# A gated recurrence on one core: the update gate's recurrent product in half precision from a split state, behind the reset gate's, and VectorE's side work in another order

## What is computed

```python
vz = video @ C_z + b_z; vr = video @ C_r + b_r; vh = video @ C + b
xz = einsum('btd,de->bte', seq, W_z)   # xr with W_r, xh with W
def step(h, xs):
    z = sigmoid(xzt + h @ U_z + vz)
    r = sigmoid(xrt + h @ U_r + vr)
    hh = tanh(xht + r * h @ U + vh)
    h_new = (1.0 - z) * h + z * hh
    return (h_new, h_new)
out = x + (all h_new, by batch and time)
```

## Time and profile before

| | |
|---|---|
| median of three runs | 2472.28 us (2469.28 to 2473.05) |
| profiled execution, its own time | 2469.78 us |
| its span, first to last instruction | 2468.0 us |
| busy: PE, DVE, ACT, POOL | 97%, 63%, 32%, 26% |
| mean granted clock of TensorE | 0.991 |

### The profile page before, as it was taken

The page is one execution under the profiler, slowest core; times in us unless marked ns, Lnnn a source line. Parts: engine busy times, 40 slices in busy tenths (PEclk is TensorE's granted clock), DMA queues, the critical chain, the costliest instruction groups (busy, mean ns, idle before and its releaser), DMA issues.

```text
span 2468.0 us, 166186 instructions
## 1 busy us (share of the span) xinstructions
PE 2390.1 (97%) x74366; PEld 2074.1 (84%) x74366; DVE 1544.1 (63%) x6617; ACT 787.9 (32%) x2571; POOL 632.5 (26%) x1165
## 2 busy tenths in 40 slices
PE   2999999999999999999999999999999999999998
PEld 1888888888888888888888888888888888888887
DVE  3666656666566665666656666566665666666665
ACT  2333333333333333333333333333333333333322
POOL 0222222222222222222222222222222222222222
PEclk8999999999999999999999999999999999999999
DMA  9010110110101101101101111011011011011000
GB/s 192 22 39 22 39 39 22 39 34 26 40 22 38 39 21 40 38 21 39 38 23 38 31 29 38 23 38 39 22 38 40 21 39 38 22 38 38 21 21 21
DMA packets 145969, 87.90 MB, mean 36 GB/s; under 512 B 9024, under 2 KB 140608, under 8 KB 145216
## 3 DMA queue, kind: packets, MB, share of 16 engines
q1 hardware_dynamic: 145216, 76.84, 12.2%
HBM read 43.25 MB, written 33.55 MB: 31 GB/s over the span
## 4 chain that ended last, share of the span: by engine, by line
PE 96%; issue 1%; SPq 1%; DVE 1%; DMA 1%; ACT 0%; POOLq 0%; POOL 0%; DVEq 0%
PE banks L208 55%; PE p_bank L216 40%; DMA w_stage<-in_L_cond_W_z_dram 1%; SPq L120 0%; SPq L115 0%; SPq L126 0%; DVE h_t L473 0%; DVE w_top L394 0%; DVE taken L467 0%; PE p_bank L224 0%; ACT gate_c L324 0%; DVE state L471 0%; DVE w_lo L407 0%; ACT w_hi L311 0%; SPq L123 0%
## 5 line engine op out<-in xcount | busy, mean ns | idle before, releaser
L216 PE MATMUL p_bank<-w_hi,x_t 128*32 128x384 f16 x16384 | 1122.1, 327 | 7.1 <-issue 7.0
L208 PE MATMUL banks<-u,h_t 128*32 128x128 f32 x32768 | 1004.1, 274 | 18.7 <-issue 16.8
L208 PEld LDWEIGHTS banks<-u,h_t 128*32 128x32 f32 x32768 | 912.9, 110 | 73.5 <-issue 23.9
L216 PE MATMUL p_bank<-w_lo,x_t 128*32 128x384 f16 x8192 | 739.2, 327 | 0.5 <-issue 0.5
L216 PEld LDWEIGHTS p_bank<-w_hi,x_t 128*32 128x32 f16 x16384 | 510.2, 97 | 115.3 <-issue 9.9
L208 PE MATMUL banks<-u,reset_t 128*32 128x128 f32 x16384 | 554.4, 274 | 2.8 <-issue 2.3
L455 DVE TENSOR_TENSOR reset<-gate_r,state 128x64 f32<-128x64 f32 x1024 | 226.7, 221 | 509.6 <-ACT gate_r L319 509.6
L208 PEld LDWEIGHTS banks<-u,reset_t 128*32 128x32 f32 x16384 | 442.2, 109 | 87.1 <-DVE reset_t L457 35.8
L187 POOL TENSOR_TENSOR result<-x_nat,state 128x128 f32<-128x128 f32 x512 | 235.4, 460 | 939.6 <-DVE state L471 939.6
L181 POOL TENSOR_TENSOR kept<-keep,state 128x128 f32<-128x128 f32 x512 | 236.0, 461 | 875.3 <-ACT keep L321 875.3
L388 DVE SCALAR_TENSOR_TENSOR banks<-p_bank,x_down,base 128x128 f32<-128x128 f32 x1536 | 429.4, 341 | 6.3 <-PE p_bank L216 4.2
(11 more groups left out here) (39 smaller groups left out, 419.9 us busy)
## 6 DMA issues: line engine op xcount, KB each, us to landing
x_nat<-in_x_dram SPq DMA_DIRECT2D x256, 128.0 KB, 2.9
out_dram<-result SPq DMA_DIRECT2D x256, 128.0 KB, 2.7
c_w<-in_L_cond_C_r_dram SPq DMA_DIRECT2D x4, 256.0 KB, 6.4
c_w<-in_L_cond_C_z_dram SPq DMA_DIRECT2D x4, 256.0 KB, 9.1
c_w<-in_L_cond_C_dram SPq DMA_DIRECT2D x4, 256.0 KB, 11.8
w_stage<-in_L_cond_W_r_dram SPq DMA_DIRECT2D x4, 256.0 KB, 14.6
w_stage<-in_L_cond_W_z_dram SPq DMA_DIRECT2D x4, 256.0 KB, 16.6
w_stage<-in_L_cond_W_dram SPq DMA_DIRECT2D x4, 256.0 KB, 17.1
```

The lines of the kernel that those rows point to most:

```text
L208: last = nc.tensor.matmul(out[part(j)], turned[:, part(q)], weights[:, q, cols(j)], start=first and q == 0, stop=q == Q - 1, skip_group_ch ...
L216: last = nc.tensor.matmul(p_bank[k][part(j), 0:G * N], x_t[set_][:, c, part(q), a], w[b][:, :, q, cols(j)], start=f == 0, stop=f == GROUPS ...
```

## The change

The update gate's recurrent matrix `U_z` is scaled and split once at the start into two float16 halves, as the input matrices were before, and loaded ahead of them. In each step ScalarE rounds the turned state to float16 (`h_hi`), VectorE makes the remainder (`h_lo`), and TensorE forms the update product from three float16 products, 48 matmuls of 128 columns, behind the reset product; the third of them waits for `h_lo`. The scale is taken out again in ScalarE's two sigmoids. Around it the side work is laid out in another way: the seed of the next step's reset gate moves to the head of VectorE's step, ahead of `h_lo`; the other two seeds stay; the scale of x is made over three steps; x is turned one time step at a time, three steps ahead, behind the seeds; and ScalarE's two passes over x stand in different steps.

```diff
-    SUM_STEPS, TOTAL_STEP, SCALE_STEP, SPLIT_STEPS, TURN_STEPS = (0, 1), 2, 3, (3, 5), (5, 7)
+    SUM_STEPS, TOTAL_STEP, POWER_STEP, UP_STEP, DOWN_STEP = (7, 0), 1, 2, 3, 4
+    WHOLE_STEPS, HIGH_STEPS, TURN_AHEAD = (3, 5), (4, 6), 3
+    UZ = G
+    SPLITS = (UZ, R, Z, C)
...
+        uz = [sb(n, [P, Q, E], f16) for n in ("uz_hi", "uz_lo")]
+        h_hi, h_lo = sb("h_hi", [P, N], f16), sb("h_lo", [P, N], f16)
...
+            load_weights(u[:, Z], U_z, s_u_in[Z])
             for g, m in enumerate((W_r, W_z, W_h)):
                 load_weights(w_stage[:, g], m, s_w_in[g])
-            for g, m in enumerate((U_r, U_z, U_h)):
-                load_weights(u[:, g], m, s_u_in[g])
+            load_weights(u[:, R], U_r, s_u_in[R])
+            load_weights(u[:, C], U_h, s_u_in[C])
...
-                if t in SPLIT_STEPS and not (last and j == BODY - 1):
-                    k = SPLIT_STEPS.index(t)
+                if t in HIGH_STEPS and not (last and j == BODY - 1):
+                    k = HIGH_STEPS.index(t)
                     rest_of_x(k, 2 * n + 3 + k if first or last else pool.snap(2 * n + (3 + k)))
...
+            def update_product(out, now):
+                pe.wait_ge(h_hi_ready, now)
+                for a, b in PARTS:
+                    if a == 1:
+                        pe.wait_ge(h_lo_ready, now)
+                    for q in range(Q):
+                        for j in range(J):
+                            last = nc.tensor.matmul(out[part(j)], (h_hi, h_lo)[a][:, part(q)], uz[b][:, q, cols(j)],
+                                                    start=False, stop=q == Q - 1, skip_group_check=True)
+                return last
...
+            for m, g in enumerate(SPLITS):
+                pe.wait_ge(s_w_top, m + 1)
+                total(p_bank[0][:, G * N + 2 + g:G * N + 3 + g], all_sum, w_top[:, g:g + 1]).then_inc(s_w_total, 1)
+                pe.wait_ge(s_w_up, m + 1)
...
-                product(cell(k, Z), h_t, u[:, Z]).then_inc(z_mm, 1)
+                update_product(cell(k, Z), now).then_inc(z_mm, 1)
...
-                    if c == 0:
-                        sets = i * (STEPS // SET) + m + 1
-                        pe.wait_ge(x_t_ready, sets if last else pe.snap(sets))
+                    pe.wait_ge(x_t_ready, s + 3 if last else pe.snap(s + 3))
                     project(k, c, 0, BEFORE_C, m % 2)
...
+            def whole_x(n, k, before):
+                if before is not None:
+                    act.wait_ge(x_lo_ready, before)
+                nc.scalar.activation(x_whole[:], x_nat[n % BUFS][:, k * SET:(k + 1) * SET], ACT.Copy,
+                                     scale=x_up[n % 2][:]).then_inc(x_whole_ready, 1)
+
...
                 if turned is not None:
                     act.wait_ge(x_t_ready, turned)
-                if before is not None:
-                    act.wait_ge(x_lo_ready, before)
-                nc.scalar.activation(x_whole[:], tile, ACT.Copy, scale=x_up[n % 2][:])
-                nc.scalar.activation(x_parts[k][:, :, 0], tile, ACT.Copy, scale=x_up[n % 2][:]).then_inc(x_hi_ready, 1)
+                nc.scalar.activation(x_parts[k][:, :, 0], x_nat[n % BUFS][:, k * SET:(k + 1) * SET], ACT.Copy,
+                                     scale=x_up[n % 2][:]).then_inc(x_hi_ready, 1)
...
+            act.wait_ge(x_in[1], 16 * J)
+            sum_x(1, 0, 2)
+            for m, g in enumerate(SPLITS):
+                act.wait_ge(s_w_up, m + 1)
+                nc.scalar.activation(split_of(g, 0), stage_of(g), ACT.Copy, scale=w_up[:, g:g + 1]).then_inc(s_w_hi, 1)
...
+                act.wait_ge(h_t_ready, HALVES * (s + 1) if last else act.snap(HALVES * s + HALVES))
+                nc.scalar.activation(h_hi[:], h_t[:], ACT.Copy, scale=2.0 ** POW).then_inc(h_hi_ready, 1)
                 act.wait_ge(r_mm, now)
                 nc.scalar.activation(gate_r[:], cell(k, R), ACT.Sigmoid).then_inc(r_gate, 1)
                 act.wait_ge(z_mm, now)
-                nc.scalar.activation(keep[:], cell(k, Z), ACT.Sigmoid, scale=-1.0).then_inc(z_keep, 1)
-                nc.scalar.activation(gate_z[:], cell(k, Z), ACT.Sigmoid).then_inc(z_gate, 1)
+                nc.scalar.activation(keep[:], cell(k, Z), ACT.Sigmoid, scale=z_minus[:]).then_inc(z_keep, 1)
+                nc.scalar.activation(gate_z[:], cell(k, Z), ACT.Sigmoid, scale=z_down[:]).then_inc(z_gate, 1)
...
+                if t == SUM_STEPS[0] and more(2):
+                    b, u_ = divmod(j + 2, BUFS)
+                    act.wait_ge(x_in[u_], count(16 * J * (i * (BODY // BUFS) + b + 1)))
+                    sum_x(j + 2, 0, count(2 * n + 4))
+                if t == SUM_STEPS[1] and more(1):
+                    sum_x(j + 1, 1, count(2 * n + 3))
+                if t in WHOLE_STEPS and more(1):
+                    k = WHOLE_STEPS.index(t)
+                    if k == 0:
+                        act.wait_ge(x_scaled, count(n + 2))
+                    whole_x(j + 1, k, count(2 * n + (2 + k)))
+                if t in HIGH_STEPS and more(1):
+                    k = HIGH_STEPS.index(t)
+                    high_x(j + 1, k, count(BLOCK * n + (SET + SET * k)))
...
+            def power_x(k, n, count):
...
+                V.tensor_reduce(x_pow[k][:], p_bank[TOTAL_STEP % 2][:, G * N:G * N + 2], AX.X, ALU.add).then_inc(x_link, 1)
                 dve.wait_ge(x_link, count(4 * n + 1))
                 exponent_of(x_pow[k][:], x_pow[k][:]).then_inc(x_link, 1)
+
+            def up_x(k, n, count):
...
-                V.tensor_scalar(x_down[k][:], w_down[:], x_pow[k][:], None, ALU.mult).then_inc(x_link, 1)
-
-            def turn_x(k, sets):
+                V.tensor_scalar(x_down[k][:], w_down[:, 0:G], x_pow[k][:], None, ALU.mult).then_inc(x_link, 1)
+
+            def turn_x(k, c, sets):
                 dve.wait_ge(x_lo_ready, sets)
...
+                V.transpose(x_t[k][:, c].rearrange("p n a -> p (n a)").bitcast(i32),
+                            x_parts[k][:, cols(c)].rearrange("p n a -> p (n a)").bitcast(i32)).then_inc(x_t_ready, 1)
+
+            def seed(k, d, gates):
+                for g in gates:
                     last = V.scalar_tensor_tensor(cell(k, g), p_bank[k][:, cols(g)], x_down[d][:, g:g + 1], base[:, g],
                                                   ALU.mult, ALU.add)
-                last.then_inc(seeded, 1)
...
+                    if g == C:
+                        last.then_inc(seeded, 1)
+
...
+            def scales_of_z():
+                link(V.tensor_copy(z_down[:], w_down[:, UZ:UZ + 1]))
+                link(V.tensor_scalar(z_minus[:], z_down[:], -1.0, None, ALU.mult))
+                link(up_of(z_up[:], w_pow[:, UZ:UZ + 1], 2 * POW))
+                link(V.tensor_scalar(base[:, Z], base[:, Z], z_up[:], None, ALU.mult))
+                dve.sem_inc(s_z_scale, 1)
...
             top_of_w(0)
-            top_of_w(1)
-            rest_of_w(0)
-            top_of_w(2)
-            rest_of_w(1)
-            rest_of_w(2)
+            scales_of_z()
+            for m in range(1, G + 1):
+                top_of_w(m)
+                rest_of_w(m - 1)
+            rest_of_w(G)
+            link(V.tensor_scalar(w_down[:, Z:Z + 1], w_down[:, Z:Z + 1], z_up[:], None, ALU.mult))
             scale_down(0)
-            dve.wait_ge(s_base, G)
             dve.wait_ge(s_bits, 2 * G)
             dve.wait_ge(x_link, 4)
             dve.wait_ge(projected, 1)
-            seed(0, 0)
+            seed(0, 0, range(G))
...
-                if more and t == SCALE_STEP:
+                ahead = (tt + 1) % 2, (tt + 1) // BLOCK % 2
+                if not (last and tt == STEPS - 1):
+                    if t == BLOCK - 1:
+                        dve.wait_ge(x_link, count(4 * n + 8))
                     dve.wait_ge(projected, count(s + 2))
-                    scale_x((j + 1) % 2, n + 1, count)
+                    seed(*ahead, (R,))
+                dve.wait_ge(h_hi_ready, now)
+                V.scalar_tensor_tensor(h_lo[:], h_t[:], 2.0 ** POW, h_hi[:], ALU.mult, ALU.subtract)\
+                    .then_inc(h_lo_ready, 1)
+                if more and t == POWER_STEP:
+                    power_x((j + 1) % 2, n + 1, count)
+                if more and t == UP_STEP:
+                    up_x((j + 1) % 2, n + 1, count)
+                if more and t == DOWN_STEP:
                     scale_down((j + 1) % 2)
-                if more and t in TURN_STEPS:
-                    k = TURN_STEPS.index(t)
-                    turn_x(k, count(2 * n + (3 + k)))
...
                 if not (last and tt == STEPS - 1):
-                    if t == BLOCK - 1:
-                        dve.wait_ge(x_link, count(4 * n + 8))
-                    dve.wait_ge(projected, count(s + 2))
-                    seed((tt + 1) % 2, (tt + 1) // BLOCK % 2)
-
+                    seed(*ahead, (Z, C))
                 dve.wait_ge(kept_ready, now)
+                if not (last and tt >= STEPS - TURN_AHEAD):
```

(5 more changed lines are left out.)

82 lines of the change are left out of this document (34 added, 48 removed).

## The result

The changed kernel took 2621.59 to 2625.96 us in three executions (a fourth, disturbed one of 8484.61 us is left out, as is one of 4221.56 us of the run with the padding apart), against 2469.28 to 2473.05 for the kernel before: a ratio of 1.0613, 95% interval [1.0592, 1.0634]. The forecast was 2481 us, its range 2441 to 2507.

What follows compares the result with a forecast made beforehand. Recurrence (2.01 us) and TensorE (2.07) were taken as nearly balanced before the candidate, TensorE bounding the rest. Blocks +5, last block −0.5, start +6, passes −3, stalls 2: together +9, 2479 profiled, median 2481 us; range 2441 to 2507.

Steps and rivals of the forecast that it cites:

- Plain step 4.51, recurrence 2.01: In steps without GpSimd's subtraction, the recurrence up to the candidate takes over at 2.01 us; the step falls 0.06 to 4.51.
- Twelve groups in 0.65 us: On TensorE, the update product's 48 float16 passes, twelve groups at 0.054 us, take 0.65 us instead of 0.87 in float32.
- The rival of slow groups: On TensorE, a float16 group takes longer than its columns: at 0.080 us plain steps are 4.66, total 2554; chance 0.10.
- Held, not shared: In two steps a block, GpSimd's subtraction blocks `h_lo` to its end: 4.91 us (chance 0.57); shared 4.62 (rival, 0.20).
- Start +6: Ahead of the steps, scaling and splitting a fourth matrix adds 6 us, between 4 and 8.
- Layout at nothing: VectorE's rearranged side work, seeds and turning x, ends at 2.00 us, hidden by nearly 0.3 before tanh ends.
- Passes −3: At seven pass starts TensorE runs at half pace; the update product saves about 0.45 us each, −3 us.
- some 2 us for stalls that TensorE's cover of 0.06 used to swallow: Last term of the sum: some 2 us for stalls that TensorE's 0.06 us of extra work a step had hidden.
- the two signs named for a failure: The forecast fails if `h_lo` is short beside the subtraction, or the twelve groups take much more than 0.65 us.

Runs made afterwards that it cites:

- the run with the padding apart: The kernel before with 16 unused two-column matmuls a step, one group of four behind every third projection group: 2611.51 us.
- the merged one: The changed kernel with the update gate's two products with h_hi merged, 32 matmuls a step instead of 48, low half's sum left out: 2497.13 us.
- the doubled padding: The kernel before with 32 unused matmuls of two columns a step behind the update gate's product: 2794.79 us.
- the run with the shortest product on TensorE: The changed kernel with GpSimd's subtraction in pieces and the update product from h_hi and U_z's high half alone, 16 matmuls: 2530.99 us.
- the one with the merged product: The changed kernel with both h_hi products merged, low half's sum left out, and GpSimd's subtraction in pieces of 128 columns: 2446.89 us.

## Why the prediction was wrong

*Plain step 4.51, recurrence 2.01:* right, 4.51 and 2.02. *Twelve groups in 0.65 us:* right; the three products of the plain step start at 1378.54, 1378.76 and 1378.98, 0.22 us apart for four groups of matmuls, 0.055 a group. The rival of slow groups is out by these rows.

*Held, not shared:* right. `h_lo` ends with the subtraction, its step takes 4.90 where 4.91 was forecast. But its worth, 49 us, shows only where the supply allows it: 0 in the changed kernel, 50 in the merged one.

*Start +6:* 7.1. *Layout at nothing:* right, by the run with the layout alone.

*Passes −3:* wrong in sign. The program jumps back six times, not seven. The six steps at these jumps took 7.56 to 8.44 us before and 8.86 to 10.17 after, 7.9 us more together; the saving on TensorE doesn't count where it waits for its instructions.

**The step that failed** is the last term of the sum, "some 2 us for stalls that TensorE's cover of 0.06 used to swallow". It measured 144 us, by the idle time of TensorE's loads put down to "issue", 8 of them at the ends of passes. I costed the twelve groups by columns, and by that 0.22 us of TensorE time was saved; I didn't count them as instructions. 64 loads and matmuls became 96, in less time, and the pace went from 15.7 to 14.0 ns. No rival covered this, and neither of the two signs named for a failure came up: `h_lo` was held and the groups were fast. A faint sign stood in the trace of before: 52.7 us of idle time put down to "issue", on TensorE's loads, and a queue that carries instructions all along. But 16 of these lie ahead of the first step and 19 at the ends of passes; only the other 17 tell of stops within a pass.

My own theory needed mending as well. A floor of 15.5 ns for every instruction missed the doubled padding (15.0) by some 50 us. Shown are the dependence on the count, its independence of the place and of what the instructions compute, the 256, and that the stops end with a packet. The median of 15.7 ns between two stops in a row is close to the pace at which the stops set in, between 15.5 and 15.0. The single ways vary from 3.51 to 5.02 us, and the excess grows by degrees. Why the next packet starts no sooner, and why the ways vary, stays open.

## What to carry to other kernels

Cost an edit on TensorE twice, by its columns and by its instructions: divide the planned step by TensorE's loads and matmuls, and where that pace gets below what the kernel runs at without "issue" stops (here 15.5 ns), a faster product gives back only a part (at 15.0 ns 38 us of 78), or nothing. Splitting one product into several narrow ones is then paid for in instructions. Halves that share a stationary operand can stand side by side in one wider matmul, which took back 125 us here; but adding the two halves up afterwards on VectorE cost more than that, so no version with the whole split product was faster than the kernel before. And gains don't add up while one limit swallows another: the removal of the lock was worth nothing in one kernel and 50 us in the next.

## What the runs showed of the hardware that was not expected

- TensorE stopped only at places 256 of its instructions apart, all 162 times, 0.62 us each on average, and each stop ended 1.17 to 1.61 us after a packet of the instruction queue.
- 16 matmuls of two columns a step, with their 16 loads, cost 153 us over 512 steps in one place and 143 in four, where the shortest steps grew by some 51 and 55 us.
- GpSimd's short instructions hold VectorE too: a 0.46 us `kept` stretched a product of 0.18 to 0.44 us, so the run with the shortest product on TensorE was 84 us slower than the one with the merged product.
- A jump back to the start of the written-out steps cost about 3.8 us here (15.0 us for four jumps fewer).
